# Softmax weight folded into the diagonal: four VectorE instructions per half head instead of a small one and a large one

## The reference, cut to what matters

```python
sx, ix = top_k(sim[0], 8); sy, iy = top_k(sim[1], 8)      # per head, 8 heads
scores, pk = top_k(sx[:, None] + sy[None, :], 8)          # 8 picks of 64 pairs
wd = down_embed[indices]; wu = up_embed[indices]          # 64 rows of 512 each
h = gelu(einsum('bnd,bnhkd->bnhk', x, wd))
h = softmax(scores) * h
out = einsum('bnhk,bnhkd->bnd', h, wu)
```

## Time and profile before

| what | value |
|---|---|
| median of the runs | 3670.32 us |
| the profiled execution's own time | 3686.62 us |
| span in that execution | 3684.8 us, 34330 instructions |
| mean granted TensorE clock | 0.918 |
| PE busy | 3065.0 us, 83% |
| DVE busy | 2444.7 us, 66% |
| ACT busy | 1723.2 us, 47% |
| POOL busy | 2062.8 us, 56% |
| gathered by POOL's DMAs | 1073.87 MB in 2048 issues |

### The profile page before, as it was taken

The page is one execution under the profiler, slowest core; times in us unless marked ns, Lnnn a source line. Parts: engine busy times, 40 slices in busy tenths (PEclk is TensorE's granted clock), DMA queues, the critical chain, the costliest instruction groups (busy, mean ns, idle before and its releaser), DMA issues.

```text
span 3684.8 us, 34330 instructions
## 1 busy us (share of the span) xinstructions
PE 3065.0 (83%) x8870; PEld 1516.5 (41%) x8870; DVE 2444.7 (66%) x5247; ACT 1723.2 (47%) x5110; POOL 2062.8 (56%) x2193
## 2 busy tenths in 40 slices
PE   8999999687778888888887878788888888888777
PEld 6778756333333333333333333333333333333333
DVE  5777735466666667666767666676666676667665
ACT  1222201455545555545545555554545555455554
POOL 1111142466666666666666666666666666666665
PEclk9999999799898989889998989898898989998989
DMA  5111101699999999999999999999999999999998
GB/s 188 58 53 60 49 17 36 246 361 367 358 367 359 368 350 368 364 371 362 360 370 357 370 359 378 347 367 367 363 367 362 363 371 363 364 355 363 367 362 314
DMA packets 324665, 1132.41 MB, mean 307 GB/s; under 512 B 36188, under 2 KB 36828, under 8 KB 323881
## 3 DMA queue, kind: packets, MB, share of 16 engines
q0 software_dynamic: 294912, 1073.87, 77.0%
q1 hardware_dynamic: 28800, 55.92, 4.3%
q10 hardware_dynamic: 808, 0.99, 0.1%
HBM read 1113.87 MB, written 16.78 MB: 307 GB/s over the span
## 4 chain that ended last, share of the span: by engine, by line
DVE 20%; another core or an unknown queue 18%; PE 15%; ACT 14%; issue 14%; POOL 2%; DMA 0%; POOLq 0%; DVEq 0%; ACTq 0%
ACT rows L1216 11%; PE expert_out_ps L1381 10%; DVE rows L1034 8%; DVE expert_diag L1048 4%; PE expert_score_ps L1360 3%; POOL rows L861 2%; DVE expert_top_s L948 2%; DVE expert_top_i L956 1%; ACT expert_act_h L1228 1%; DVE expert_coef L1040 1%; PE expert_out_ps L1295 1%; ACT L1228 1%; DVE expert_best_i L979 1%; DVE expert_onehot L1017 1%
## 5 line engine op out<-in xcount | busy, mean ns | idle before, releaser
L861 POOL DMA_INDIRECT rows<-in_table,expert_idx x2048 | 1936.8, 946 | 1116.3 <-issue 626.0
L1381 PE MATMUL expert_out_ps<-rows,expert_diag 128*128 128x512 f32 x4096 | 2026.6, 646 | 540.6 <-DVE expert_diag L1048 214.3
L1216 ACT ACTIVATE rows<-rows 128x512 f32<-128x512 f32 x2048 | 1261.6, 617 | 932.3 <-DVE expert_coef L1040 501.5
L1381 PEld LDWEIGHTS expert_out_ps<-rows,expert_diag 128*128 128x128 f32 x4096 | 830.4, 207 | 1685.6 <-issue 1267.6
L1034 DVE TENSOR_TENSOR rows<-rows,expert_xn_ps 128x2048 f32<-128x2048 f32 x512 | 1167.0, 2279 | 36.5 <-DMA rows<-in_table,expert_idx 19.6
L1040 DVE TENSOR_TENSOR expert_coef<-expert_act_h,expert_prob 128x4 f32<-128x4 f32 x512 | 82.3, 161 | 833.5 <-remote 467.2
L1360 PE MATMUL expert_score_ps<-amat,expert_xnT 128*128 128x512 f32 x992 | 473.3, 601 | 17.7 <-issue 9.9
L1216 ACT ACTIVATION_READ_ACCUMULATOR rows<-rows 128x1 f32 x2048 | 382.2, 187 | 0.8 <-issue 0.8
L1048 DVE TENSOR_TENSOR expert_diag<-expert_bias_ps,expert_coef 128x512 f32<-128x512 f32 x512 | 348.9, 681 | 36.8 <-remote 19.5
L1360 PEld LDWEIGHTS expert_score_ps<-amat,expert_xnT 128*128 128x128 f32 x992 | 189.2, 191 | 261.3 <-issue 248.9
L1228 ACT ACTIVATE expert_act_h<-expert_hid 128x4 f32<-128x4 f32 x512 | 105.1, 205 | 347.2 <-remote 280.7
(11 more groups left out here) (129 smaller groups left out, 1812.9 us busy)
## 6 DMA issues: line engine op xcount, KB each, us to landing
rows<-in_table,expert_idx POOLq DMA_INDIRECT x2048
x_t<-in_x SPq DMA_DIRECT2D x32, 256.0 KB, 2.9
attention_xr_t<-in_x SPq DMA_DIRECT2D x32, 256.0 KB, 2.8
x_dram<-rows SPq DMA_DIRECT2D x32, 256.0 KB, 2.0
expert_x_t<-x_dram SPq DMA_DIRECT2D x32, 256.0 KB
out_y<-expert_x_t SPq DMA_DIRECT2D x32, 256.0 KB
rows<-in_w_q SPq DMA_DIRECT2D x4, 1024.0 KB, 7.0
rows<-in_w_qT SPq DMA_DIRECT2D x4, 1024.0 KB, 9.1
```

Of the source, the lines that this page charges most:

```text
L861: pool.indirect_dma_start(rows[:, k % SLOTS, :], None, table[:, :], bass.IndirectOffsetOnAxis(ap=idx[:, par, k:k + 1], axis=0))\
L1216: ins = act.activation(down, down, ACT.Copy, accum_out=hid[:, j % RING, k:k + 1])
L1381: mm = pe.matmul(out_ps[:, par, :], diag[:, j % RING, k, :], rows[:, j % GROUPS * HALF + k, D:2 * D], start=(j == 0 and k == 0), stop=(j = ...
```

## The change

The coefficients are no longer made. Each of the four diagonals of a half head is one instruction of its own, `scalar_tensor_tensor`: identity (PSUM) times gelu (one value per partition) times softmax weight (one value per partition, read 128 times with stride zero). The four stand directly behind the products of the next half head, ahead of the extras, where the coefficients stood. The semaphore `coef_done` goes. `multiplied` is now incremented by the products of every half head, and ACT waits for it before its sums. The waits for gelu and for `up_done` of four half heads before both stand ahead of the four.

```diff
--- before.py
+++ after.py
@@ -760,7 +760,6 @@
     prob = sb("prob", [P, 2, NPICK])
     hid = sb("hid", [P, RING, HALF])
     act_h = sb("act_h", [P, RING, HALF])
-    coef = sb("coef", [P, RING, HALF])
     score_ps = ps("score_ps", [P, 2, 512])
     turn_ps = ps("turn_ps", [P, KC, P])
     xn_ps = ps("xn_ps", [P, 2, D])
@@ -776,7 +775,7 @@
     keys_in = sem("keys_in")
     issued = sem("issued")
     ev = {n: sem(n) for n in """xn_done turned xnT_done scored seeded topped early_done shifted
-        exp_done idx_done multiplied summed ident_kept gelu_done coef_done diag_done up_done y_done consts yw_done var_done
+        exp_done idx_done multiplied summed ident_kept gelu_done diag_done up_done y_done consts yw_done var_done
         mean_done var_eps rs_done scale_made offset_made offset_done raw_done normed scaled bias_done
         bias_kept a_done amat_done flagged offset_wide""".split()}
 
@@ -1034,21 +1033,16 @@
                 return dve.tensor_tensor(
                     down, down, xn_ps[:, par, :].unsqueeze(1).to_broadcast([P, HALF, D]), ALU.mult)
 
-            def coefficients(t, par, j):
+            def diagonals(t, par, j):
 
                 wait(dve, "gelu_done", t * HALVES + j + 1)
-                dve.tensor_tensor(coef[:, j % RING, :], act_h[:, j % RING, :],
-                                  prob[:, par, j * HALF:(j + 1) * HALF], ALU.mult)\
-                   .then_inc(ev["coef_done"], 1)
-
-            def diagonals(t, j):
-
-                wait(dve, "coef_done", t * HALVES + j + 1)
                 wait(dve, "up_done", t * HALVES + j + 1 - RING)
-                dve.tensor_tensor(diag[:, j % RING, :, :],
-                                  ident_ps.unsqueeze(1).to_broadcast([P, HALF, P]),
-                                  coef[:, j % RING, :].unsqueeze(2).to_broadcast([P, HALF, P]),
-                                  ALU.mult).then_inc(ev["diag_done"], 1)
+                for k in range(HALF):
+                    at = j * HALF + k
+                    ins = dve.scalar_tensor_tensor(
+                        out=diag[:, j % RING, k, :], in0=ident_ps, scalar=act_h[:, j % RING, k:k + 1],
+                        in1=prob[:, par, at:at + 1].to_broadcast([P, P]), op0=ALU.mult, op1=ALU.mult)
+                ins.then_inc(ev["diag_done"], 1)
 
             def finish(t, par, half):
 
@@ -1059,15 +1053,13 @@
             def step(t, par, half, more, first):
                 for j in range(HALVES):
                     dve.wait_ge(row_in[j % GROUPS], half * 256 + (par * 2 + j // GROUPS + 1) * 64)
-                    made_products = products(par, j)
-                    if first and j == 0:
-                        made_products.then_inc(ev["multiplied"], 1)
+                    products(par, j).then_inc(ev["multiplied"], 1)
                     if j in (4, 6, 11, 14) and more >= 2:
                         wait(dve, "scored", (t + 2) * NQ + (4, 6, 11, 14).index(j) + 1)
                     if j > 0:
-                        coefficients(t, par, j - 1)
+                        diagonals(t, par, j - 1)
                     elif not first:
-                        coefficients(t - 1, 1 - par, HALVES - 1)
+                        diagonals(t - 1, 1 - par, HALVES - 1)
                     if j == 0:
                         if more >= 1:
                             top_places(3)
@@ -1132,10 +1124,6 @@
                             weights(1 - par)
                         if more >= 2:
                             pair_places(0)
-                    if j > 0:
-                        diagonals(t, j - 1)
-                    elif not first:
-                        diagonals(t - 1, HALVES - 1)
 
             made = 0
 
@@ -1191,8 +1179,7 @@
             norm(2, 0, 1)
             wait(dve, "ident_kept", 1)
             run(step)
-            coefficients(NT - 1, 1, HALVES - 1)
-            diagonals(NT - 1, HALVES - 1)
+            diagonals(NT - 1, 1, HALVES - 1)
             finish(NT - 1, 1, NT // 2 - 1)
 
         @block.scalar
@@ -1218,11 +1205,7 @@
 
             def step(t, par, half, more, first):
                 for j in range(HALVES):
-
-                    if first and j == 0:
-                        wait(act, "multiplied", 1)
-                    else:
-                        wait(act, "coef_done", t * HALVES + j)
+                    wait(act, "multiplied", t * HALVES + j + 1)
                     sums_of_products(j)
                     wait(act, "summed", t * HALVES + j + 1)
                     act.activation(act_h[:, j % RING, :], hid[:, j % RING, :], ACT.Gelu_apprx_tanh)\
```

## The result

The changed kernel takes 3669.14 us, the median of 20 runs (3660.76 to 3676.3); the kernel before took 3661.61 us on the same chip, also in 20 runs (3653.27 to 3671.23). The ratio is 1.0015, 95% interval [1.0008, 1.0022]: some 5 us slower (7.5 us between the medians), less than the 0.3% at which the prediction put "no change", but clear of noise. The forecast was 3656 us and faster. It had been set against 3670.32 us, the median of three of the runs of before; against the median of all 20, 0.4% less would be 3647 us. The profiled execution has a span of 3663.2 us and an own time of 3665.04 us. It is not to be held against the 3686.62 us of the profiled execution before, which lies outside the 20 runs of before and was presumably taken on another chip; the profiles of before and after are therefore compared in kind, and sums of waits only roughly.

The account below looks back on a forecast made before the run. POOL's gather issues and its waits for `up_done` were taken to bound the kernel. From the profiled 3686.6 us, 14 us for earlier diagonals gave 3673; 16 us lower for the median of runs gave 3656 us, range 3612 to 3728.

Parts of the forecast that it names:

- DVE's term: On DVE, four new instructions of 0.26 us replace 0.66 us of work: 0.38 us longer per half head, 195 us in all.
- The cover: DVE's idle time ahead of the coefficients, 833.5 us, would absorb its added work, which would then cost nothing.
- the conversion of PE's earlier start: On PE, diagonals 0.76 us earlier at 119 waits become progress per cycle: 125 POOL waits instead of 129, -14 us.
- The unit: On POOL, a cycle of 23.2 us: 129 waits of 3.5 us, one per 3.97 half heads.
- The floor: POOL's gather issues, 4.98 us for each of 512 half heads: 2550 us that the change doesn't touch.
- ACT's freedom: ACT, released by the products instead of the coefficients, was taken to gain nothing; bounds 0 and 223.7 us.
- Rival D: ACT's earlier release removes DVE's 223.7 us of waits for gelu: -42 us, 3628 us; chance 0.10.
- Rival B: No change: POOL's release follows its own stop, so earlier diagonals on PE are hidden too; 3670 us; chance 0.25.
- C: Slower: DVE's longer work sets how far a cycle gets, 141 POOL waits, +42 us, 3712 us; chance 0.27.
- A: The forecast itself: PE's earlier diagonals save 14 us of POOL's waits; 3656 us, own range 3635 to 3668; chance 0.38.

Follow-up runs that it names:

- Part 9: No new run: counts over the traces; POOL's next gather came a median of 11.1 us after PE's last matmul before the change, 10.1 us after it.
- the light kernel: The kernel before with products, sums and up matmuls over 64 of 512 columns, four gathers per half head, on the fourth chip: 3345.1 us, ratio 0.9961.

## Why the prediction was wrong

*DVE's term was right.* 4 x 0.26 us was predicted, 1.04 us was measured; DVE's busy time rose from 2444.7 to 2640.8 us, 196 us against the 195 predicted. The duration, 344 ns, lies in the middle of the 280 to 404 that the two nearest rows gave as bounds.

*The cover was nearly right.* "Cost nothing" became about 10 us for 195 and 29 us for 615, both estimated across chips, and both a twentieth.

*The step that failed is the conversion of PE's earlier start.* The prediction took 119 waits x 0.76 us, called it 0.70 us of progress per cycle, and made 125 waits out of 129, "-4 x 3.5 = -14 us". PE's waits named after the diagonals did shrink (279.1 to 194.7 us), but with "remote", as the prediction counted them, they grew (417 to 483 us), its idle time before the matmuls did too (540.6 to 584.1 us), and moving the diagonals by itself gained 0.1% with an interval that reaches 1. The premise under it was already in doubt in the prediction's own reading: it said that the release follows POOL's stop and not PE's end, and then priced PE's progress all the same. Part 9 has the size: POOL goes on a median of 11 us after the matmul that it needs, so 0.76 us gained by PE is far inside that time. The unit was rough as well: POOL's waits were 97 of 3.5 us and 67 of 1.7 us, 164 in all and not 129, one per 3.1 half heads. The stops sum to what is missing between 1.243 us per issue and the 1.45 us of pace, 0.2 us per gather; that is bookkeeping. What the experiments add is that this remainder hardly moves whatever DVE, PE, the bytes, the rows or the increments of ACT and PE do, and however it is cut into stops. The floor of 512 x 4.98 = 2550 us was too low for the same reason; the kernel with half its products and up matmuls shows 2048 x 1.44 = 2950 us, and the kernel before stood within 18 us of that one's time.

*ACT's freedom* was worth nothing by the prediction and 0.9995 [0.9985, 1.0004] by the run: right. Rival D falls. Rival B (no change, since the release follows POOL's own stop) had the mechanism; that its 3670 us is so near the measured 3669.14 is luck, as it stood for the 3661.61 us of before. C's sign was right and its size not (+12 waits, +42 us; measured some 5 us, and 152 waits against 164 in profiles of presumably different chips). The measured time lies inside the stated 3612 to 3728 us, and just above the 3635 to 3668 that A had for itself.

*The result* would then be the sum of two small terms that nearly cancel: about -0.1% for order and ACT's wait, about +0.3% for the four instructions. The second was obtained by subtraction, so this split is an estimate and not a test.

*What stays open* is why increments arrive late on three chips and in the result's pair, whether it is POOL's stream of gathers that holds them up, and whether the increments that each gather makes have a part in it. That the late ones mostly arrive in POOL's stops, and that DVE's idle stretches of over 4 us end in such a stop or in the issue just before it in 29 of 44 cases of the changed kernel, speaks for POOL's stream, but no run tests it. Whether the fourth chip is free of them by itself or by the light kernel isn't separated either; its kernel before, with the full compute, is only 0.4% slower than the light one, which speaks for the chip.

## What to carry to other kernels

When a stage issues one instruction many times, divide a window's length by their count before you believe the spacing of its issues. If that pace doesn't move when you lighten each other engine, as here, don't count the waits of the issuing engine as room for improvement. Before you price a wait, measure how long ago the work that it waits for had ended: 11 us here, against a gain of 0.76. A cycle whose length nobody has explained may not be used as an exchange rate for time saved elsewhere. In this kernel only the number of gathers moved the time by much: cutting the compute's columns to an eighth was worth 0.4%, leaving out one gather in four 19%.

## What the runs showed of the hardware

- A gather of 128 rows of 4 KB has a pace of 1.44 to 1.47 us on three chips (341 to 347 in 500 us), the same for 2 KB rows and for 64 rows, while the issue lasts 0.95 us (0.91 with 64 rows) with 0.30 us behind it. On a fourth chip, beside an eighth of the compute's columns, it is 1.30 to 1.32 us at 410 GB/s.
- On the three chips semaphore increments are recorded late: in the kernel before 228 of the 412 recorded increments by PE's up matmuls stand more than 1 us after the matmul, the one by the score matmul in the timeline above 13.9 us. On the fourth chip it is 1 of 501.
- The DMA share of 0.96 alone is no sign that the DMA sets the pace: with half the bytes it was 0.64 and the time the same.
- `scalar_tensor_tensor` of 128x128 from PSUM with one value per partition as scalar and another read with stride zero: 344 ns, spaced 0.26 us.
- PE lighter by half its columns in the up matmuls had a mean granted clock of 0.80 in the window and not 0.91; its busy time fell from 402 to 290 us.
